# A two-layer decoder on one Trainium2 core: rounded integers kept in bf16 between VectorE's two passes

## What is computed

```python
def qa(x, s):                        # activations: integers from -128 to 127
    return jnp.clip(jnp.round(x / s), -128.0, 127.0)
x_q = qa(layernorm(x), S_IN)
wq, ws = qw(in_proj_w)               # weights: integers too
proj_q = qa(x_q @ wq.T * (S_IN * ws), S_Z)
hs_q, gate_q = proj_q[:Din], proj_q[Din:]
conv_out = depthwise_conv(hs_q, cwq) * (S_Z * cws) + conv_b
u_q = qa(silu(conv_out), S_U)
```

## Time and profile before

| what | us |
|---|---|
| median of 3 runs | 3856.45 (3853.66 to 3860.16) |
| the profiled execution, its own time | 3849.94 |
| its span, first to last instruction | 3848.2 |
| busy in the span: TensorE | 3296.1 (86%) |
| VectorE | 2539.0 (66%) |
| ScalarE | 1754.5 (46%) |
| GpSimd | 1072.2 (28%) |
| mean granted clock of TensorE | 0.928 |

### The profile page before, as it was taken

One profiled execution on the slowest core, in us unless ns is written; L12 is line 12 of the kernel. 1 busy time (PEld: TensorE's weight loads), 2 busy tenths in 40 slices (PEclk: granted clock), 3 DMA queues, 4 the chain that ended last, 5 costly groups with the idle time before them and its releaser, 6 DMA issues. The chain is left out here.

```text
span 3848.2 us, 38078 instructions
## 1 busy us (share of the span) xinstructions
PE 3296.1 (86%) x12741; PEld 1716.7 (45%) x12741; DVE 2539.0 (66%) x4790; ACT 1754.5 (46%) x3290; POOL 1072.2 (28%) x697
## 2 busy tenths in 40 slices
PE   2751499999999799999999998792999699999964
PEld 2330244444444455455554555441444345655552
DVE  7778899999998555555555555434111768877654
ACT  3657566666665343333433334241101227767521
POOL 0343699999996010101000000123000200000014
PEclk9875799999999899999999998796999899999967
DMA  6114435353532222222111211244000200000046
GB/s 211 68 57 133 162 98 145 99 145 94 136 99 97 71 63 66 77 72 72 58 55 52 63 50 61 80 128 137 0 0 0 82 0 1 1 1 1 1 138 217
DMA packets 180499, 297.65 MB, mean 77 GB/s; under 512 B 23761, under 2 KB 74321, under 8 KB 176977
## 3 DMA queue, kind: packets, MB, share of 16 engines
q1 hardware_dynamic: 167232, 261.48, 21.2%
q0 software_dynamic: 12208, 33.57, 3.3%
q10 hardware_dynamic: 864, 0.18, 0.0%
HBM read 198.55 MB, written 96.60 MB: 77 GB/s over the span
## 5 line engine op out<-in xcount | busy, mean ns | idle before, releaser
L1201 POOL TENSOR_TENSOR sc_dBu<-sc_dtu,xa 128x1024 f32<-128x1024 f32 x256 | 540.0, 2131 | 38.2 <-DMA sc_dtu<-scan_dtu 29.0
L1111 PE MATMUL y_ps<-sc_g,ident 128*128 128x512 f32 x1024 | 476.2, 600 | 18.6 <-POOL sc_g L1189 12.1
L1225 DVE TENSOR_TENSOR_SCAN sc_dA<-sc_dA,sc_dBu 128x1024 f32<-128x1024 f32 x160 | 365.1, 2282 | 6.4 <-POOL sc_dBu L1201 6.4
L1451 ACT ACTIVATE c_p<-c_ps,c_sm 128x512 f32<-128x512 f32 x256 | 195.6, 774 | 352.6 <-DVE c_sm L1492 352.6
L1165 ACT ACTIVATE sc_dA<-sc_dt,a_neg 128x511 f32<-128x511 f32 x512 | 329.6, 676 | 11.1 <-DVE sc_g L1225 9.8
L1491 DVE TENSOR_REDUCE c_sm<-c_ps 128x4 f32<-128x2048 f32 x64 | 146.7, 2292 | 275.2 <-PE c_ps L1414 275.2
L1111 PEld LDWEIGHTS y_ps<-sc_g,ident 128*128 128x128 f32 x1024 | 189.8, 190 | 256.6 <-issue 168.1
L1484 DVE SCALAR_TENSOR_TENSOR xa<-c_ps,c_sm,xa 128x512 f32<-128x512 f32 x256 | 192.1, 751 | 147.1 <-PE c_ps L1405 133.5
L1405 PE MATMUL c_ps<-c_wo,c_oT 128*128 128x512 f32 x512 | 246.5, 605 | 2.3 <-DVE xa L1484 1.6
L1386 PE MATMUL c_ps<-c_xT,c_wq 128*128 128x512 f32 x512 | 232.3, 597 | 5.2 <-DMA c_wq<-in_c_wq_dram 5.2
L1433 PE MATMUL c_ps<-c_pT,c_v 128*128 128x512 f32 x512 | 232.0, 596 | 2.1 <-DVE c_pT L1503 2.1
(11 more groups left out here) (490 smaller groups left out, 6306.7 us busy)
## 6 DMA issues: line engine op xcount, KB each, us to landing
kv_w<-in_c_wkv_dram SPq DMA_DIRECT2D x32, 512.0 KB, 4.1
cross_keys<-kv_out SPq DMA_DIRECT2D x64, 256.0 KB, 2.0
cross_values<-kv_out SPq DMA_DIRECT2D x128, 128.0 KB, 1.9
c_kT<-cross_keys SPq DMA_DIRECT2D x64, 256.0 KB, 2.7
c_rk<-cross_rk SPq DMA_DIRECT2D x64, 256.0 KB, 3.3
c_v<-cross_values SPq DMA_DIRECT2D x64, 256.0 KB, 2.7
expert_rows<-e_yt SPq DMA_DIRECT2D x63, 256.0 KB, 2.0
xa<-scan_bc SPq DMA_DIRECT2D x48, 256.0 KB, 7.9
```

The costliest lines, as they stand in the source:

```text
L1111: ins = pe.matmul(yps[:, k % 2, :], ident[:], g[:, c % GS, n, :], start=False, stop=(m == NCH - 1 and n == NG - 1))
L1201: pool.tensor_tensor(dBu[:, c % 3], spread(dtu[:, k % DT, :], NG), bc[:, m * NG:(m + 1) * NG, :], ALU.mult).then_inc(s_dBu, 1)
L1225: dve.tensor_tensor_scan(to.rearrange("p n s -> p (n s)"), dA[:, c % 2].rearrange("p n s -> p (n s)"), dBu[:, c % 3].rearrange("p n s -> p ...
L1451: ins = act.activation(pr[:, j, :], ps[:, SB + j, :], ACT.Exp, scale=rq[:, j:j + 1], bias=bias[:, j:j + 1], accum_out=l[:, j:j + 1])
```

## The change

In the entry the rounding pass comes first: it reads one of now two f32 buffers and writes one of four new bf16 buffers `xb`; the clamp is done there in place, on bf16. TensorE transposes bf16 with the bf16 identity into a bf16 PSUM tensor, and the copies read bf16. ScalarE's tile t waits for VectorE's rounding of tile t-2 instead of the transposes of t-4; that wait for t-4 is now VectorE's, ahead of the pass that writes `xb`.

In the projection the first pass subtracts MAGIC, clamps at 127 and writes the bf16 destination; the second clamps at -128 in place there. The number of instructions stays as it is.

```diff
-        xn = sb("xn_m", [P, R, H])
+        xn = sb("xn_m", [P, 2, H])
+        xb = sb("xb_m", [P, R, H], BF16)
...
-        ps = ctx.enter_context(nc.psum_tensor("nps_m", [P, R, H], F32))
+        ps = ctx.enter_context(nc.psum_tensor("nps_m", [P, R, 2 * H], BF16))
...
-                        ins = pe.transpose(ps[:, t % R, c * P:(c + 1) * P], xn[:, t % R, c * P:(c + 1) * P], ident[:])
+                        ins = pe.transpose(ps[:, t % R, c * P:(c + 1) * P], xb[:, t % R, c * P:(c + 1) * P], identb[:])
...
-                        if t >= R:
-                            act.wait_ge(s_tr, t - R + 1)
-                        act.activation(xn[:, t % R, :], xa[:, t, :], ACT.Identity, scale=rs[:, 2, t:t + 1],
+                        if t >= 2:
+                            act.wait_ge(s_xn, t - 1)
+                        act.activation(xn[:, t % 2, :], xa[:, t, :], ACT.Identity, scale=rs[:, 2, t:t + 1],
                                        bias=rs[:, 0, t:t + 1]).then_inc(s_ap, 1)
...
-                        v = xn[:, t % R, :]
-                        own.after(dve.tensor_scalar(v, v, -128.0, 127.0, ALU.max, ALU.min))
-                        dve.tensor_scalar(v, v, MAGIC, MAGIC, ALU.add, ALU.subtract).then_inc(s_xn, 1)
+                        v = xb[:, t % R, :]
+                        if t >= R:
+                            dve.wait_ge(s_tr, t - R + 1)
+                        own.after(dve.tensor_scalar(v, xn[:, t % 2, :], MAGIC, MAGIC, ALU.add, ALU.subtract))
+                        dve.tensor_scalar(v, v, -128.0, 127.0, ALU.max, ALU.min).then_inc(s_xn, 1)
...
-                    own.after(dve.tensor_scalar(v, v, MAGIC - 128.0, MAGIC + 127.0, ALU.max, ALU.min))
                     if what == "hs":
-                        ins = dve.tensor_scalar(hs[:, i, :, PAD:PAD + S], v.rearrange("p (b s) -> p b s", b=NB), MAGIC, None,
-                                                ALU.subtract)
+                        to, v = hs[:, i, :, PAD:PAD + S], v.rearrange("p (b s) -> p b s", b=NB)
                     else:
-                        dst = gate if what == "gate" else u
-                        ins = dve.tensor_scalar(dst[:, i, :], v, MAGIC, None, ALU.subtract)
-                    ins.then_inc(s_d, 1)
+                        to = (gate if what == "gate" else u)[:, i, :]
+                    own.after(dve.tensor_scalar(to, v, MAGIC, 127.0, ALU.subtract, ALU.min))
+                    dve.tensor_scalar(to, to, -128.0, None, ALU.max).then_inc(s_d, 1)
```

More of the change, by code:

```diff
@@ L244, in mamba @@
                 xq = sb("xq", [P, HC, T], BF16, c3)
-                entry(nc, A, x_dram, xa, xq, u, gate, wq, cw, cb, dtb, dsk, a_neg, lnw, mx, mxa, winv, wsc, kk, rmw, zero, ident)
+                entry(nc, A, x_dram, xa, xq, u, gate, wq, cw, cb, dtb, dsk, a_neg, lnw, mx, mxa, winv, wsc, kk, rmw, zero, ident, identb)
                 hs = sb("hs", [P, CT, NB, PAD + S], BF16, c3)
@@ L253, in mamba, with entry @@
         out_proj(nc, x_dram, xa, gate, owq, kk, ssk, kv[2])
-def entry(nc, A, x_dram, xa, xq, u, gate, wq, cw, cb, dtb, dsk, a_neg, lnw, mx, mxa, winv, wsc, kk, rmw, zero, ident):
+def entry(nc, A, x_dram, xa, xq, u, gate, wq, cw, cb, dtb, dsk, a_neg, lnw, mx, mxa, winv, wsc, kk, rmw, zero, ident, identb):
     table, locu, tot = rmw[:3]
@@ L401, in _ @@
                         act.activation(xq[:, :, (t - 2) * P:(t - 1) * P],
-                                       ps[:, (t - 2) % R, :].rearrange("p (c t) -> p c t", c=HC), ACT.Copy).then_inc(s_ea, 1)
+                                       ps[:, (t - 2) % R, 0:H].rearrange("p (c t) -> p c t", c=HC), ACT.Copy).then_inc(s_ea, 1)
             @block.vector
@@ L490, in _ @@
                         dve.tensor_copy(xq[:, :, (t - 2) * P:(t - 1) * P],
-                                        ps[:, (t - 2) % R, :].rearrange("p (c t) -> p c t", c=HC)).then_inc(s_ed, 1)
+                                        ps[:, (t - 2) % R, 0:H].rearrange("p (c t) -> p c t", c=HC)).then_inc(s_ed, 1)
                 dve.wait_ge(s_cnt, 1)
```

## The result

The changed kernel takes 3838.5 us, median of 20 runs (3832.01 to 3849.86). The kernel before, run beside it and before, now has a median of 3850.26 us over 20 runs (3842.35 to 3860.16); the first three of them had 3856.45. The ratio, taken between runs made side by side, is 0.9973, with a 95% interval from 0.9964 to 0.9982: 10.4 us faster, between 7 and 14. The two medians are 11.8 us apart.

A forecast was written before the change was run, and what follows sets the result against it. The projection stage was taken as set by GpSimd's chain of 14 table updates, held back by VectorE, and the entry's loop as nearly ScalarE-bound. Gains of 2.6 + 5.9 = 8.5 us from the 3856.45 median gave 3847.9; range 3843 to 3855.

The forecast's parts named there:

- The passes: VectorE's second rounding pass, bf16 to bf16: 0.70 us at 2048 elements, saving 0.53 us a round; 0.30 at 512.
- a second pass that is no faster: Rival: the 16-bit second pass gains nothing, the entry gains 1 us from TensorE; 3855.5 us, chance 0.06.
- The entry: Loop over 16 tiles at the entry's end: quicker transposes and passes bring its end 2.6 us earlier, low end about 0.
- The moved waits: Entry loop: the new waits of ScalarE and VectorE were to cost nothing in this order.
- The projection: Stage of input projection and convolution: GpSimd's chain of 14 table updates is held less, gaining 5.9 us, low end 0.
- Holding: GpSimd's chain in the projection: time GpSimd is held back during VectorE's wide instructions, 26.1 us over 42 instructions.
- The first rival: The projection's chain does not shorten, through chance meetings and landings behind 1 MB stores; 3853.9 us, chance 0.17.
- The rule of the square: Projection: GpSimd's delay under VectorE goes with the square of pass length, 34% less per round, giving 5.9 us.
- busy time: Projection alternative: GpSimd's delay goes only with how long VectorE is busy, giving 3.7 us.
- What is late next: Projection's end: ScalarE's last gate store, 7.3 us ahead of GpSimd's last scatter, moves forward about as much as the chain.
- Nearly all holding under one-input passes: Rival in the projection: one-input passes' share is close to 1, not 0.66, so 8.9 us there; 3845.0 us, chance 0.18.
- A slow clock in the projection: Rival: TensorE stays at 1.2 GHz in the projection, making it 23 us slower; 3871 us, chance 0.05.

The follow-up runs named there:

- The second profile of the changed kernel: The changed kernel run once more with nothing altered: projection section 129.8 us, ratio to the kernel before 0.9972 (0.9956 to 0.9989).
- dropping the remainders: The changed kernel without the projection's eight two-input VectorE passes that take the weights' remainders: section 125.6 us, ratio to the kernel before 0.9973 (0.9959 to 0.9988).

## Why the prediction was right and wrong

*What failed is the base, not a cost.* "Sum" and "How the numbers follow" took the forecast and its range from the median of three runs, 3856.45, and put into the range only the bounds of the change's terms. That median was 6.2 us above the one of 20 runs, which includes these three, and in the later batches the kernel before had medians from 3844.7 to 3848.7. The text had the warning: the profiled execution lay 6.5 us below the median, which it called "at the fast side of runs that spread over 6.5 us"; it lay in fact 3.7 us below the fastest of the three. Three runs that scatter by that much do not fix a median to 2 us; whether these three were chance or the chip was slower at the time isn't known. From 3850.26 the same 8.5 us give 3841.8, and the range 3836.8 to 3848.8, which holds 3838.5. Of the 9.4 us between the forecast and the time, 6.2 are the base; the other 3.2 are a gain larger than 8.5, of which the sections place 0.2. The scatter of the base belonged into the range as a term of its own.

*The passes.* 0.70 us was taken, 0.694 measured (0.85 and 0.54 were the bounds); in the entry 0.30 against 0.294, the copy 0.40 against 0.419. The rival of a second pass that is no faster is refuted by its rows, with the gaps too.

*The entry.* The steps came as worked out: the first ACT copy at 99.94 (99.8), VectorE's last at 114.20 (114.0), 2.6 us forecast and 2.5 measured (the steps as written add up to 2.74: 2.45 for the start and 0.29 for the copy). The moved waits cost nothing to be seen: VectorE waited once for the transposes, 0.67 us at 101.27, and ScalarE ran without idling up to its last copy.

*The projection.* 5.9 us forecast, 6.1 measured, but by a sum that hides two errors, so the near match is luck. Holding fell by 8.9 us, not 5.9: by a third of all of it, where the working had a third of two thirds. Against that, the chain lost 2.7 us in waits for its own transfers (5.0 more for scatters, 2.3 less for gathers), which the sum had put at nothing. The second profile of the changed kernel has both larger, 11.5 us less holding and 6.3 more waiting, and the chain comes out 5.2 us shorter instead of 6.3. The first rival had this mechanism, as what would undo the whole gain; it undid a third to a half of what the holding gave back. That the longer waits come from 1 MB stores ahead of the scatters is argued from their place, and was not tried alone. The rule of the square is neither shown nor refuted: removing the second pass shortened the section by 1.9 us, where the square gave 3 and busy time 5; doubling it made the chain no longer (0.1 us), where they gave 3 and 5; dropping the remainders brought 3.4 of 5. All are below what either rule says, since part of what the holding gives or takes goes into the waits.

*What is late next.* The chain stayed last in the changed kernel, as forecast. The last store is issued 7.8 us ahead of its last scatter (7.3 before), so this path moved forward by 6.7 us, about as much as the chain, as forecast too. It takes over once two steps are gone.

*The rivals.* The chain did shorten (first). Nearly all holding under one-input passes (second) gave 3845.0, for a gain of 11.5 us, near the measured one, and 8.9 us less holding, just what the first profile shows. That is luck: its mechanism is refuted by the remainders, without which GpSimd is busy 3.3 to 5.9 us less. The prediction took from the Trainium skill, SBUF — State Buffer, "Who interferes with whom", that the two-input passes would hold the issues less. The Trainium skill says there that a two-input pass contends with GpSimd instructions that read SBUF, and not with those that only write it. The rows above agree with it (held at 164.34, 2.78 us instead of 0.98, and not at 214.86), if an issue reads SBUF as it begins, for the indices `locu` that stand behind its arrow; that this is the reason is an inference. "Less" was right, "nearly nothing" was not. A slow clock in the projection (fourth) did not come: TensorE had 72.24 us busy there at 0.88, against 73.54 at 0.87. (Its 3871 is 23 us added to the profiled execution; from the median that the other rivals use it would be 3877.)

*The size.* The chance of a gain above 0.2% was 0.48; it came, at 0.27%, with an interval from 0.18% to 0.36%.

## What to carry to other kernels

When a section ends in a barrier, look for the engine that is last, even if the change is on another: here faster passes of VectorE paid through GpSimd, whose table updates they hold back, and moving two of those updates to sections with room shortened this one by as much again. Watch the last engine's waits as well as its busy time: what the holding gave back, collisions with the stores took in part. A second pass that is 16-bit on both sides cost 0.69 us here, against 1.23 for one over f32. And take the scatter of the base as a term of the range: three runs told the median to some 6 us, as much as the change was worth.

## What was not expected of the hardware

TensorE's granted clock in the two norm and gate sections took one of three means, 0.66, 0.57 or 0.52, from one profile to the next with the same instructions, and with it 41, 47 or 50 us. In the 46 us behind the projection it was 0.65 before and after. A scatter's issue of 0.98 us can last 3.43 us under two VectorE passes in a row with 0.03 us between them: the gap is not enough for GpSimd to finish. It depends on the kind of the second pass: 0.86 us were enough beside another two-input pass (164.34), while a one-input pass held the issue until 0.12 us behind its own end (181.14). And a second pass of little over half the length did not bring the chain forward by all that GpSimd was held less: 8.9 us less held, 2.7 us more waited.
